# Feed-forward with block quantization: a second buffer for ScalarE's scaled copy, and another place for the addition in VectorE's queue

## The reference, cut to what matters

```python
def fp4_quant_dequant(x):                      # in blocks of 16 numbers of a row
    xb = x.reshape(shape[:-1] + (shape[-1] // 16, 16))
    scale = jnp.maximum(jnp.max(jnp.abs(xb), axis=-1, keepdims=True) / 6.0, 1e-12)
    idx = jnp.searchsorted(_MID, jnp.abs(xb / scale))
    return (_GRID[idx] * jnp.sign(xb / scale) * scale).reshape(shape)

def fp4_linear(x, w):
    return jnp.einsum('bsk,nk->bsn', fp4_quant_dequant(x), fp4_quant_dequant(w))

h = silu(fp4_linear(x, w_gate)) * fp4_linear(x, w_up)      # 352 wide
x = x + fp4_linear(h, w_down)                              # x inside is normalised
```

## Time and profile before

| | |
|---|---|
| median of three runs | 1463.47 us |
| lowest, highest | 1460.0, 1467.11 us |
| profiled execution | 1465.41 us |
| its span, first to last instruction | 1463.7 us |
| mean granted TensorE clock | 0.905 of full speed |
| busy TensorE / VectorE / ScalarE / GpSimd | 80% / 64% / 31% / 35% |

### The profile page before, as it was taken

How to read it: one execution, slowest core, us unless ns; L and a number is a source line. 1 busy time by engine, 2 the same in 40 slices (tenths; PEclk the granted TensorE clock), 3 DMA queues, 4 the chain that set the end, 5 groups by cost and what they waited for, 6 DMA issues and landing times.

```text
span 1463.7 us, 16561 instructions
## 1 busy us (share of the span) xinstructions
PE 1172.7 (80%) x4825; PEld 699.6 (48%) x4825; DVE 939.5 (64%) x2037; ACT 446.6 (31%) x844; POOL 507.3 (35%) x461
## 2 busy tenths in 40 slices
PE   3899999905656564699999889999988997399990
PEld 1444444403345432355555555555555665277770
DVE  5787888775577699467667556766754665323324
ACT  3545444235322231222122322212232322133340
POOL 4788888922244156400000000000000366245552
PEclk9999999957977785699999999999999998599995
DMA  4312222000000003100008200000000112434415
GB/s 134 107 56 63 76 63 77 1 0 1 1 0 0 1 0 137 65 22 22 14 21 355 74 0 22 22 14 21 8 15 7 44 50 68 125 87 112 121 46 183
DMA packets 60188, 81.82 MB, mean 56 GB/s; under 512 B 8620, under 2 KB 34622, under 8 KB 59617
## 3 DMA queue, kind: packets, MB, share of 16 engines
q1 hardware_dynamic: 55201, 72.54, 15.6%
q0 software_dynamic: 4672, 8.55, 1.8%
q10 hardware_dynamic: 256, 0.03, 0.0%
HBM read 33.77 MB, written 31.99 MB: 45 GB/s over the span
## 4 chain that ended last, share of the span: by engine, by line
PE 65%; DVE 16%; issue 8%; POOL 4%; ACT 4%; DMA 1%; SPq 1%; DVEq 0%; POOLq 0%; ACTq 0%
PE banks L1516 45%; PE banks L1405 7%; PE banks L1551 2%; PE banks L1337 2%; PE banks L1338 2%; PE banks L1493 1%; DVE arena L1990 1%; PE banks L1467 1%; DVE X L1878 1%; PE banks L1346 1%; POOL arena L936 1%; DVE arena L1798 1%; ACT XN L1158 1%; POOL arena L971 1%; DVE q_small L649 1%
## 5 line engine op out<-in xcount | busy, mean ns | idle before, releaser
L1516 PE MATMUL banks<-arena 128*128 128x128 f32 (+4 forms) x1516 | 391.5, 397 | 7.6 <-DVE arena L2084 4.5
L1516 PEld LDWEIGHTS banks<-arena 128*128 128x128 f32 (+1 forms) x1516 | 208.8, 191 | 89.2 <-issue 61.6
L1405 PE MATMUL banks<-arena,ident 128*128 128x512 f32 x368 | 175.3, 609 | 10.3 <-DVE arena L1829 9.0
L1022 POOL IOTA arena<- 128x32 f32 x1 | 0.2, 205 | 510.2 <-DVE ttt_val_w L2091 510.2
L2029 DVE TENSOR_TENSOR arena<-banks,arena 128x512 f32<-128x512 f32 x64 | 44.2, 691 | 134.4 <-ACT arena L1228 134.4
L936 POOL TENSOR_TENSOR arena<-arena 128x512 f32<-128x512 f32 x96 | 112.2, 1195 | 16.8 <-ACT arena L1095 16.8
L1054 POOL DMA_INDIRECT expert_out_scratch<-arena x80 | 80.6, 1007 | 97.1 <-DVE arena L2286 76.0
L1405 PEld LDWEIGHTS banks<-arena,ident 128*128 128x128 f32 x368 | 67.7, 194 | 88.2 <-issue 64.9
L1829 DVE TENSOR_TENSOR arena<-arena,banks 128x512 f32<-128x512 f32 x152 | 96.1, 675 | 0.5 <-PE banks L1405 0.5
L943 POOL TENSOR_TENSOR arena<-arena 128x512 f32<-128x512 f32 x64 | 81.3, 1270 | 5.0
L1231 ACT ACTIVATE arena<-banks 128x512 f32<-128x512 f32 x64 | 38.2, 597 | 146.5 <-PE banks L1551 146.5
(11 more groups left out here) (316 smaller groups left out, 2122.7 us busy)
## 6 DMA issues: line engine op xcount, KB each, us to landing
arena<-arena SPq DMA_DIRECT2D x64, 224.0 KB
arena<-expert_in_scratch SPq DMA_DIRECT2D x16, 580.5 KB
expert_in_scratch<-arena SPq DMA_DIRECT2D x4, 1225.5 KB
expert_in_scratch<-arena SPq DMA_DIRECT2D x5, 967.5 KB
arena<-kT_scratch SPq DMA_DIRECT2D x16, 256.0 KB, 2.6
arena<-k_scratch SPq DMA_DIRECT2D x16, 256.0 KB, 2.6
arena<-in_L_ffn_W_dram SPq DMA_DIRECT2D x16, 256.0 KB, 3.0
arena<-expert_out_scratch SPq DMA_DIRECT2D x8, 512.0 KB, 6.8
```

What stands on the lines that cost most here:

```text
L1405: m = nc.tensor.matmul(bank[ACC[b % 2]][:], ident[:], src, start=first, stop=last)
L1516: return nc.tensor.matmul(out_, lhsT, rhs, start=start, stop=stop)
```

## The change

`q_tmp` gets a sixth part, and ScalarE's scaled copy of piece k goes to part 0 or part 5 as k is even or odd; `round_small(k)` waits for `level_add(k - 2)` instead of `level_add(k - 1)`, and `level_add(k)` reads the part that fits. In VectorE's loop of the second half `add_down(k - 10)` stands behind `level_bits(k)` instead of ahead of `block_maxima(k + 1)`.

```diff
-        q_tmp = view(o4, 5, QN)
+        q_tmp = view(o4, 6, QN)
...
         def round_small(act, k):
             act.wait_ge(scaled_down.sem, scaled_down.at(k + 1))
-            if k:
-                act.wait_ge(level_step.sem, level_step.at(3 * (k - 1) + 2))
+            if k >= 2:
+                act.wait_ge(level_step.sem, level_step.at(3 * (k - 2) + 2))
             n = 16 * shape_of(k)[0] * shape_of(k)[1]
-            nc.scalar.activation(q_tmp[:, 0, 0:n], scaled_value(k), ACT.Copy, scale=1.0 / SMALL).then_inc(small_ready.sem, small_ready.unit)
+            nc.scalar.activation(q_tmp[:, 5 * (k % 2), 0:n], scaled_value(k), ACT.Copy, scale=1.0 / SMALL).then_inc(small_ready.sem, small_ready.unit)
...
             for k in range(NB, 2 * NB):
-                if k >= NB + 2:
-                    add_down(k - NB - 2)
                 if NB + 2 <= k + 1 < 2 * NB:
                     block_maxima(dve, k + 1)
                 level_bits(dve, k)
+                if k >= NB + 2:
+                    add_down(k - NB - 2)
                 level_add(dve, k)
                 level_less(dve, k)
```

More of the change, by code:

```diff
@@ L244, in build @@
         WNc = sb("WNc", P, 3 * FC, P)
-        q_tmp = view(o4, 5, QN)
-        assert o4 + 5 * QN <= 30000
+        q_tmp = view(o4, 6, QN)
+        assert o4 + 6 * QN <= 30000
         q_small = sb("q_small", P, 8, QN // 16)
@@ L681, in level_add @@
             dve.wait_ge(small_ready.sem, small_ready.at(k + 1))
-            nc.vector.scalar_tensor_tensor(by_tiles_of(scaled_value(k)), steps_of(k), 1.5, by_tiles_of(q_tmp[:, 0, 0:n]), ALU.max, ALU.add).then_inc(level_step.sem, level_step.unit)
+            nc.vector.scalar_tensor_tensor(by_tiles_of(scaled_value(k)), steps_of(k), 1.5, by_tiles_of(q_tmp[:, 5 * (k % 2), 0:n]), ALU.max, ALU.add).then_inc(level_step.sem, level_step.unit)
         def level_less(dve, k):
```

## The result

The changed kernel takes 1448.58 us, median of four runs (1447.38 to 1451.84), against 1463.89 (1460.0 to 1467.11): a ratio of 0.9899 with a 95% interval of 0.9878 to 0.9919. The forecast was 1450, between 1444 and 1457. The profiled execution took 1447.38 us, its span is 1445.6.

What follows compares the result with a forecast made beforehand. A ring of waits, no engine full, sets the pace in the feed-forward's second half. Saving 13.7 us gives 1451.7 from the profiled 1465.41, or 1449.8 against the median 1463.47: forecast 1450, 8 in 10 between 1444 and 1457.

Steps and rivals of the forecast that it cites:

- VectorE paces, turn 9.05: Feed-forward's second half: VectorE never waits in the new turns, each 9.05 us instead of 11.49; chance 0.75.
- D in the middle: add_down placed between level_bits and level_add on VectorE: costs 0.48 us a turn, at most its own 0.69.
- L651's stall in every turn: block_maxima's second step, beside GpSimd's scaled_back, takes 1.17 us instead of 0.20: 0.95 more in every turn.
- Rival (b): L651 in block_maxima does not stall in the five new turns, 4.8 us more won: 1445; chance 0.07.
- Part 1: Two buffers for ScalarE's scaled copy: alone they take 0.6 us off a turn, to 10.9.
- part 2: add_down moved behind level_bits on VectorE: block_maxima and level_bits no longer stand behind the wait for the product.
- 3.0 us to spare: TensorE's product, slow clock, is ready at 11.25 us; add_down asks at 14.3, counted from block_maxima's start.
- Rival (e): add_down waits in VectorE's pass and delays the next transposes: 1471 with a product 7 us late; chance 0.05.
- The tail: Groups 6 and 7 at the stage's end: the last add_down starts 11.6 to 14.3 us earlier, taken as 13.7.
- both groups fast: Groups 6 and 7 on TensorE at the fast clock, 5.0 us each: 14.3 us won.
- group 7 slow: Group 7 on TensorE at the slow clock, group 6 fast: 13.1 us won.
- What lies behind: Statistics, normalised tiles and q/k/v products hang on the last add_down, so the whole 13.7 us passes on.

Runs made afterwards that it cites:

- e3: The changed kernel with block_maxima(k + 1) moved behind level_bits(k): 1510.41 us, 0.9892 of the kernel before on the same chip; a second time 0.9919.
- e4: The changed kernel with VectorE's block maxima written to PSUM, where L651 reads them: 1507.09 us, 0.9875 of the kernel before; a second time 0.9872.
- e2: The changed kernel with add_down back ahead of block_maxima, so only the second buffer is new: 1519.72 us, 0.9953 of the kernel before.
- e1: The kernel before with only add_down moved behind level_bits, the scaled copy keeping one buffer: 1512.54 us, 0.9908 of the kernel before.
- e7b: The changed kernel with two more ScalarE copies behind round_small per group, holding the product back 2.7 us: 1520.85 us, 0.9936 of the kernel before.
- e8b: The changed kernel with five more ScalarE copies behind round_small per group, holding the product back 6.9 us: 1546.66 us, 1.0119 of the kernel before.
- after_again: The changed kernel run again without an edit on another chip: 1512.06 us, 0.9899 of the kernel before.
- e5: On top of e3, bn_stats of the first 24 tiles put ahead of add_down(6): 1510.34 us, 0.9902 of the kernel before.

## Why the prediction was right

- **VectorE paces, turn 9.05.** Measured 9.02. The D in the middle costs 0.48 (B to A 2.13, without it 1.65), as estimated.
- **L651's stall in every turn.** Right, 1.17 five times more, and shown by e3 and e4: it goes when M is moved away from SB, and also when L651 reads from PSUM while SB runs. Rival (b) falls.
- **Parts.** Part 1 was estimated at 0.6 of a turn by itself, from 11.5 down to 10.9 at the slow clock; e2 has 10.91 where the product took 2.93, and 0.6 less than before in every turn when the product is taken off. That the other turns are 9.6 to 10.1 is the product, which took 1.6 to 2.2 there. The estimate left out that the kernel before had such products too: its turns are 10.7 to 11.5, 11.26 in the mean, and not all 11.5. The forecast did not rest on that, as it was counted from S(15) and the last D as they stood. That part 2 makes part 1 needless, which the prediction's own sum implies (even at 7.5 + 1.3 + 0.5 + 2.9 = 12.2 the product is ahead of 14.3), I didn't say there; e1 shows it.
- **3.0 us to spare.** Right as far as e7b goes, which shows no wait at 2.7 us later. For products that are late in every group a second limit, which the prediction did not have, lies close by, the ring of e8b: 9.02 - 6.4 = 2.6 us at 1.2 GHz. Rival (e) priced the turn well: longer by what exceeds 3.0 us, 12.95 for 6.9 us late; measured 13.0 to 13.3. It priced the stage too low: (6.9 - 5.45) x 5 = 7.3 us slower than before, measured 14.0 (184.4 against 170.4). It counted the turns from 11.5, which were 11.26, and left out that the first D is late too, at 433.53 instead of 426.47. Such a lateness was not near, so the forecast did not suffer.
- **The tail.** Group 7 took 4.9 us on TensorE at the fast clock, as forecast (5.0). Group 6 started at the slow one and took 6.3, between my 5.0 and 7.2; D(6) waited 3.22 instead of 2.5 and set the end through the statistics. S(9) to last D shortened by 13.4 in place of 13.7. That these lie so close is in part luck: 13.7 was set between both groups fast and group 7 slow, and what came, group 6 slow and group 7 fast, was not among the cases. In after_again both were fast, and L1158 to last D is 14.8 shorter than before, where the forecast had 14.3 for that case.
- **What lies behind.** I said that the whole passes on. Nothing of it was given back, and the first profile had 1.4 us more ahead of the stage and 3.3 behind it that no step of the prediction has; 2.3 of these are the clock at the start of the training, which two more profiles of the same kernel have on one side and on the other. The median lies 1.4 below the forecast, within what this leaves open.

What stays open is why e3, which shortens the stage by 4.5 to 6 us, shows 1.7 in the medians twice, while e5 with the same stage shows 4.3, and e4 7.5 for 6.8 in the stage. The executions behind one such median, four to six of them, spread over up to 7 us, and this scatter may be all there is to it; no run separates it from a cause behind the stage.

## What to carry to other kernels

Where an instruction waits at the head of an in-order queue for a result two groups old, work out when it is ready and when it would be asked for further down; if there is time to spare, moving it may give everything that a second buffer elsewhere promises, and the buffer then nothing. Count the spare time in every ring that goes through the waiting queue, not only in the one being loosened. And an engine that no longer rests meets its neighbours at other moments: look in the trace for an instruction whose length depends on what runs beside it.

## What the runs showed of the hardware

- A tensor_scalar of VectorE from SBUF to SBUF (128x88) took 0.20 us alone and 1.17 beside a GpSimd tensor_tensor, ending 0.06 us after it; from PSUM it took 0.25 beside the same instruction. A reciprocal from SBUF to SBUF was not held (0.70 both ways), nor were the level passes, which have one side in PSUM (1.62 beside `round_divide`, 1.62 clear of it).
- TensorE's clock rose at different moments behind the same idle of 7.4 to 7.5 us: in profiles of one and the same kernel the ten us that end the first tile of the training had a granted clock of 0.51 or of 0.91, and its first 20 matmuls took 10.3 or 8.0 us.
- The chips differ: the kernel before took 1463.9 us on the first and 1525 to 1529 on the others. In the profiles most of the difference lies in the experts: from the first to the last start of L1054, 140.8 us on the first chip and 192 to 199 on the others, while the changed kernel's turns were 9.02 us on each. Why is not shown.
